# Loads of x and stores of y move from the SyncE queue to GpSimd, at the end of its step

## The reference: what is computed

```
f = _ln(f, g1, b1)
f = jnp.roll(f, (-SS, -SS), axis=(1, 2))
win = _window_partition(f)
qkv = win @ w_qkv + b_qkv
...
attn = jax.nn.softmax(attn.reshape(-1, NH, L, L), axis=-1)
out = jnp.einsum('bhij,bhjd->bihd', attn, v).reshape(-1, L, C)
out = out @ w_proj + b_proj
...
f = residual + f.transpose(0, 3, 1, 2)
m = _ln(f.transpose(0, 2, 3, 1), g2, b2)
m = jax.nn.gelu(m @ w_fc1 + b_fc1, approximate=False) @ w_fc2 + b_fc2
return f + m.transpose(0, 3, 1, 2)
```

## Time and profile before

| | us |
|---|---|
| median of 3 runs | 3298.38 |
| lowest and highest run | 3273.74, 3312.33 |
| the profiled execution | 3292.7 |
| its span | 3290.8 |

### The profile page before, as it was taken

The page is one execution under the profiler, slowest core; times in us unless marked ns, Lnnn a source line. Parts: engine busy times, 40 slices in busy tenths (PEclk is TensorE's granted clock), DMA queues, the critical chain, the costliest instruction groups (busy, mean ns, idle before and its releaser), DMA issues.

```text
span 3290.8 us, 136960 instructions
## 1 busy us (share of the span) xinstructions
PE 2926.7 (89%) x53060; PEld 2338.7 (71%) x53060; DVE 2430.1 (74%) x7208; ACT 2070.5 (63%) x3208; POOL 1453.1 (44%) x1832
## 2 busy tenths in 40 slices
PE   1789999899998899989998999989999899999997
PEld 0677777777776777767776777767777777777775
DVE  5677777677776777767777777767777677777775
ACT  0366666566666666656666666666666566666664
POOL 2444444344444444444444444444444444444444
PEclk9799999899999999999999999999999999999999
DMA  1667777677776777767777777767767677777772
GB/s 40 170 170 187 182 190 188 164 172 184 185 175 171 176 183 193 186 164 186 189 180 175 177 178 194 184 164 186 187 168 186 164 188 179 188 186 192 182 183 71
DMA packets 409846, 573.07 MB, mean 174 GB/s; under 512 B 58376, under 2 KB 384350, under 8 KB 384365
## 3 DMA queue, kind: packets, MB, share of 16 engines
q1 hardware_dynamic: 409148, 563.72, 68.9%
HBM read 385.92 MB, written 175.21 MB: 171 GB/s over the span
## 4 chain that ended last, share of the span: by engine, by line
PE 40%; DMA 26%; issue 11%; SPq 10%; DVE 9%; ACT 4%; POOL 0%; DVEq 0%; POOLq 0%; ACTq 0%
DMA kbd<-k_image 24%; PE psum L451 10%; PE psum L384 9%; PE psum L419 5%; PE psum L435 4%; PE psum L492 4%; PE psum L477 4%; DVE nat L778 3%; DVE nmax L736 3%; ACT xfh L635 3%; SPq L292 2%; SPq L256 2%; SPq L293 2%; SPq L294 2%; PE psum L527 2%
## 5 line engine op out<-in xcount | busy, mean ns | idle before, releaser
L623 ACT ACTIVATE probs<-psum 113x784 f32<-113x784 f32 x768 | 632.2, 823 | 847.4 <-PE psum L435 844.2
L736 DVE TENSOR_REDUCE nmax<-psum 113x16 f32<-113x784 f32 x768 | 745.6, 971 | 316.5 <-PE psum L419 316.2
L347 POOL TENSOR_SCALAR ve<-mv 98x8 f32<-98x8 f32 x264 | 64.1, 243 | 1687.7 <-DVE mv L765 1687.7
L451 PE MATMUL psum<-vbd,probs 128*49 128x18 f32 x24576 | 656.5, 199 | 26.3 <-issue 25.5
L451 PEld LDWEIGHTS psum<-vbd,probs 128*49 128x49 f32 x24576 | 646.0, 128 | 32.0 <-issue 31.7
L419 PE MATMUL psum<-kbd,nat 128*49 128x196 f16 x6144 | 412.5, 254 | 114.5 <-DMA kbd<-k_image 103.8
L435 PE MATMUL psum<-qbd,kst 128*49 128x196 f16 x6144 | 413.7, 254 | 67.0 <-DVE xfl L771 45.5
L354 POOL TENSOR_TENSOR rs<-ve,half 98x8 f32<-98x8 f32 x264 | 439.5, 1665 | 0.0
L760 DVE BATCH_NORM_STATS2 st<-tok 98x6 f32<-98x96 f32 x2112 | 363.7, 245 | 80.8 <-ACT tok L630 67.3
L359 POOL TENSOR_TENSOR xn<-xn,rs 98x768 f32<-98x768 f32 x264 | 387.8, 1469 | 72.7 <-POOL rs L354 72.7
L419 PEld LDWEIGHTS psum<-kbd,nat 128*49 128x49 f16 x6144 | 269.4, 105 | 209.2 <-DMA kbd<-k_image 134.4
(11 more groups left out here) (83 smaller groups left out, 5343.1 us busy)
## 6 DMA issues: line engine op xcount, KB each, us to landing
kbd<-k_image SPq DMA_DIRECT2D x256, 882.0 KB, 6.8
stack_pages<-nat SPq DMA_DIRECT2D x256, 294.0 KB, 3.0
kst<-stack_pages SPq DMA_DIRECT2D x256, 220.5 KB
qbd<-stack_pages SPq DMA_DIRECT2D x1024, 55.1 KB
stack_pages<-nat SPq DMA_DIRECT2D x256, 147.0 KB, 3.7
xr<-in_x_dram SPq DMA_DIRECT2D x224, 147.0 KB, 3.6
out_dram<-yr SPq DMA_DIRECT2D x224, 147.0 KB, 6.3
k_image<-nat SPq DMA_DIRECT2D x256, 73.5 KB
```

The lines of the kernel that those rows point to most:

```text
L451: last = nc.tensor.matmul(dst[:, :, h, :], probs[:, b.c % 2, h // 4, p, h % 4 * L:(h % 4 + 1) * L], vbd[:, b.c % 4, p * NH + h, :, :], sta ...
L623: nc.scalar.activation(probs[0:PR, b.c % 2, u, :, :].rearrange("j (g q) k -> j g (q k)", g=2), psum[0:PR, B:B + 2, 0:2 * CH], ACT.Exp).the ...
L736: nc.vector.tensor_reduce(dst, psum[0:PR, A:A + 2, 0:2 * CH].rearrange("i g (q h j) -> i g q h j", q=2, j=L), axis=AX.X, op=ALU.max, negat ...
```

## The change

The two functions that load x and store y are taken out of SP's program and put into POOL's. POOL's step becomes: `normalise`, `order_x`, the load of x, and in odd steps the two stores of y. The waits are the same, and so are slots, semaphores and sizes. The waits for the last stores move to POOL's end too.

```diff
@@ SP
-            def load_x(b):
-                wait(sp, x_ordered, b.count(1, -3))
-                alone(sp)
-                for at, row, rows in image_rows(b):
-                    sp.dma_start(xr[:, b.c % 4, at:at + rows, :], x[b.image(), :, row:row + rows, :]).then_inc(x_in[b.c % 8], 16)
...
-            def store_y(b):
-                sp.wait_ge(y_made, b.count(1, 1))
-                alone(sp)
-                for at, row, rows in image_rows(b):
-                    sp.dma_start(out[b.image(), :, row:row + rows, :], yr[:, b.c % 2, at:at + rows, :]).then_inc(y_out[b.c % 8], 16)
...
             def step(t):
-                for offset, stage in ((LOAD, load_x), (KEYS, key_blocks)):
+                for offset, stage in ((KEYS, key_blocks), (STACK, stacks), (SCORE, maxima), (QK, save_parts)):
                     if has(t.step(offset)):
                         stage(t.step(offset))
-                if odd(t):
-                    for offset in STORE:
-                        if has(t.step(offset)):
-                            store_y(t.step(offset))
-                for offset, stage in ((STACK, stacks), (SCORE, maxima), (QK, save_parts)):
-                    if has(t.step(offset)):
-                        stage(t.step(offset))
@@ POOL
+            def load_x(b):
+                for at, row, rows in image_rows(b):
+                    nc.gpsimd.dma_start(xr[:, b.c % 4, at:at + rows, :], x[b.image(), :, row:row + rows, :]).then_inc(x_in[b.c % 8], 16)
+
+            def store_y(b):
+                pool.wait_ge(y_made, b.count(1, 1))
+                alone(pool)
+                for at, row, rows in image_rows(b):
+                    nc.gpsimd.dma_start(out[b.image(), :, row:row + rows, :], yr[:, b.c % 2, at:at + rows, :]).then_inc(y_out[b.c % 8], 16)
...
                 if has(t.step(ORDER)):
                     order_x(t.step(ORDER))
+                if has(t.step(LOAD)):
+                    wait(pool, x_ordered, t.step(LOAD).count(1, -3))
+                    alone(pool)
+                    load_x(t.step(LOAD))
+                for offset in STORE:
+                    if odd(t) and has(t.step(offset)):
+                        store_y(t.step(offset))
```

More of the change, by code:

```diff
@@ L314, in _ @@
             steps(sp, step)
-            for n in range(8):
-                sp.wait_ge(y_out[n], X_IN[n] * images)
         @block.gpsimd
@@ L366, in step @@
                     order_x(t.step(ORDER))
+                if has(t.step(LOAD)):
[5 more added lines that the diff above has]
+                        store_y(t.step(offset))
             steps(pool, step)
+            for n in range(8):
+                pool.wait_ge(y_out[n], X_IN[n] * images)
         @block.tensor
```

## The result

The changed kernel takes 3481.97 us (median of 4 runs, 3477.82 to 3485.75), the kernel before 3292.15 beside it (4 runs, 3273.74 to 3312.33). The ratio is 1.0575, with a 95% interval of 1.0508 to 1.0641. Measured once more, with fresh runs of the kernel before, it was 1.0533 (1.0463 to 1.0603). The ratios leave disturbed runs out, among them one of 5674.27 us with the keys first and one of 8871.42 us of the kernel before. The forecast was 3285, no change, with a range up to 3385: wrong, and on the slow side of all its cases.

A forecast was written before the change was run, and what follows sets the result against it. Bound: PE's wait for the key load before L419, 103.8 us. Issue on SP -50, x's data -17, y's data +55, ends +4 sum to -8, so 3292.7 becomes 3285 us; range 3210 to 3385.

The forecast's parts named there:

- What lengthens it costs all of it: PE's wait for the keys before L419: any lengthening of this path lengthens the kernel by as much.
- The stores' bytes: DMA engines, odd step: the second y delays the keys PE waits for by 0.5 us a pair, +55 us.
- P: POOL's queue: time to issue one DMA, taken as 1.0 us, between 0.34 and 1.47.
- the second rival: L419, odd step: stores served ahead of the keys, 1.24 us a pair, 3385 us; chance 0.18.
- SP's issue: SP's queue: without the load of x the keys go out up to 0.7 us sooner, -50 us.
- the bytes of x: DMA engines: x goes out earlier, no longer just ahead of the keys; 0.15 us each, -17 us.
- POOL and its cover: POOL's idle time, 4.77 us after an odd step, covers three issues of 3 us; next normalise unchanged, zero.
- DVE would hold up the descriptors: POOL's DMA issues: each might grow by part of a DVE operation; steady POOL durations spoke against it.
- The ring of y: DVE's L800 wait for y's slot: nothing, covered by 0.6 us; as a rival 3362 us, chance 0.12.

The follow-up runs named there:

- keys first: The kernel before, with SP issuing the keys ahead of the load of x instead of behind it: 3261.54 us, ratio 0.989.
- stores early: The changed kernel, with the stores of y at the start of POOL's odd step, ahead of normalise: 3291.36 us, ratio 1.003.

## Why the prediction was wrong, step by step

- **"What lengthens it costs all of it"**, the rate of one us for one us, is the step that failed. Between the variant with the stores early and the changed kernel PE's wait for the keys grew by 180.2 - 94.9 = 85 us and the span by 3482.6 - 3279.1 = 204. Of the rest, PE's busy time grew by 3063.3 - 2933.6 = 130, and its other idle time shrank by 11. No case of the prediction had TensorE's clock in it, so the range ended at 3385. Against the kernel before, the 76.4 us of longer wait alone would have made 3292.7 + 76 = 3369, inside the range; the 136.6 us of longer busy time took it out. There was a reason to ask: the mean wait was 0.94 us but the longest 3.3, and the change would lengthen waits from there. The rate does not hold for a gain either: with the keys first the wait fell by 67.8 us and the span by 37.7 (3290.8 to 3253.1).
- **The stores' bytes**, +55 us. As a delay they were sized well: 0.5 us a pair predicted, 11.17 - 10.56 = 0.61 measured against the stores early. The picture was off: with P at 0.51 to 0.65 instead of 1.0, POOL is through with both issues at about the time the keys go out. In the trace some 98 of 136 records (medians, those of 4 bytes counted in) of POOL's queue near a critical load start ahead of the keys' first packet, which comes 1.96 us after the issue and not 1.01; 38 fall in between the keys' own. The collision was the second rival (chance 0.18); its mechanism is the right one, its price without the clock was 3385. Its sign, a wait for the keys of over 200 us, was nearly met with 180.2.
- **SP's issue**, -50 us, and **the bytes of x**, -17. Both failed in the changed kernel: with the loads alone on POOL the ratio is 0.998. The keys did go out 1.0 us sooner, but landed 0.85 us later from their issue; their first packet started 1.58 us after it and not 1.01, and about 120 of the 147 KB of x started between 1 us before the issue and that packet (medians). With keys first, where the x stands behind, 0.67 us of the whole time was gained and the ratio was 0.989 (0.981 to 0.998), about half of the 67 us (2%) of the sum, which lies just outside the interval.
- **The two rules of the Trainium skill.** That the DMA engines take their queues in turn (the Trainium skill's page "DMA: Bandwidth & Descriptors", § Queues, rings and completion order) fits the 38 records among the keys' own. The rule of the same page's § Issuing engines are not separate DMA queues, that a move saves issue time only, would have given 3247; the measurement, 3482, decides against using it alone: the move also changed what lies ahead of what.
- **POOL and its cover**: right. `normalise` still waited in all 264 turns, in 219 of them for DVE's statistics, and 1 to 3 issues of 0.51 to 0.65 us fit in. That DVE would hold up the descriptors (the Trainium skill's page "SBUF — State Buffer", § SBUF: two separate sides) does not show in POOL's issues: L316 took 512 to 605 ns in all 288 cases.
- **The ring of y**: right; 7.0 us of waits, and no change with 4 slots that the intervals show.

## What to carry to other kernels

A DMA that nobody waits for still has a place in time, and moving it to another engine's program gives it a new one: look up when that engine reaches the line, and which transfer with a waiting PE is issued in the same microseconds. A longer wait of PE can cost more than its length, here 204 us for 85, since the clock may fall after it; a few useless matmuls in the wait tell the two costs apart. Here the gain lay in keeping a short queue ahead of the critical load, not in which engine issues.

## What the runs showed of the hardware

- POOL issued a DMA of 96 rows of 1568 bytes in 0.51 to 0.65 us, against a median of 0.34 on SP. Of its queue's 26624 records (77.11 MB) 14336 are of 4704 bytes, three rows joined, and 9216 of 4 bytes; SP's queue carried such rows one by one, in records of 1568 bytes.
- TensorE's clock fell to half after waits of 1.99 and 1.49 us in the two examples above, while the waits of 0.94 us on the mean in the kernel before mostly left it alone: 5 low stretches begin within 2.5 us behind one of its 111 waits for the keys, 42 behind one of the changed kernel's 127.
- Packets of a second queue whose issue began 1.13 us before the keys' went for the most part ahead of them (98 of 136 records), and stores that stood behind the keys in the same queue did not delay them (6.58 us from issue to landing, against 6.91).
